# Where the group norm is scaled, and who ends the late rotary units, in an attention + RWKV + FFN kernel

## The reference, cut to what matters

```python
x = x + attn_a(layernorm(x))       # 16 heads of 16, rotary q and k, causal softmax
x = x + ffn(layernorm(x))          # int weights, 256 -> 768 -> 256, silu(gate) * up
x = x + attn_b(layernorm(x))       # RWKV-6, 4 heads of 64
x = x + ffn(layernorm(x))

def _apply_rope(t):                # q and k
    rot = concatenate([-t2, t1])   # the halves of each head, swapped
    return t * cos + rot * sin
# attn_b ends, per token and head, with a group norm, an affine map and a gate:
y = _wkv6(r, k, v, w, u)
y = (y - mean) / sqrt(var + eps)   # over the 64 channels of a head
y = y * ln_g + ln_b
out = (y * g) @ Wo
```

## Time and profile before

| | us |
|---|---|
| median of 3 runs | 3526.66 |
| lowest, highest | 3525.41, 3527.14 |
| the profiled execution's own time | 3525.63 |
| its span, first to last instruction | 3523.5 |

### The profile page before, as it was taken

One profiled execution on the slowest core, in us unless ns is written; L12 is line 12 of the kernel. 1 busy time (PEld: TensorE's weight loads), 2 busy tenths in 40 slices (PEclk: granted clock), 3 DMA queues, 4 the chain that ended last, 5 costly groups with the idle time before them and its releaser, 6 DMA issues.

```text
span 3523.5 us, 47199 instructions
## 1 busy us (share of the span) xinstructions
PE 2997.0 (85%) x17056; PEld 1840.7 (52%) x17056; DVE 2507.5 (71%) x5137; ACT 1309.5 (37%) x2721; POOL 1308.2 (37%) x1244
## 2 busy tenths in 40 slices
PE   2588889889888898888988888888888888898898
PEld 1236565365743567345763447535475364653667
DVE  5676687677775867857778577785687756876665
ACT  1263223722346232453225531265313642236322
POOL 0023551235512454124641346213462234522355
PEclk9699999999999999899998999899998999999999
DMA  4600033000410006000150002400023000330000
GB/s 133 105 2 13 19 61 56 1 13 19 79 39 10 14 10 97 20 14 10 25 101 2 14 9 46 80 2 13 18 46 71 2 13 19 49 68 2 1 1 13
DMA packets 68887, 115.04 MB, mean 33 GB/s; under 512 B 10795, under 2 KB 64075, under 8 KB 65531
## 3 DMA queue, kind: packets, MB, share of 16 engines
q1 hardware_dynamic: 68627, 111.51, 15.9%
HBM read 74.69 MB, written 33.65 MB: 31 GB/s over the span
## 4 chain that ended last, share of the span: by engine, by line
PE 49%; DVE 34%; POOL 5%; issue 4%; ACT 4%; DMA 2%; SPq 0%; DVEq 0%; POOLq 0%; ACTq 0%
DVE mxp L928 9%; PE PB L1266 7%; PE PB L1251 5%; PE PB L1326 5%; PE PB L1341 5%; PE PB L1237 4%; DVE arena L1111 4%; PE PB L1411 3%; PE PB L1380 3%; DVE attn L851 3%; PE PB L1299 3%; DVE arena L1120 2%; ACT arena L699 2%; DVE stats L840 2%; PE PB L1450 2%
## 5 line engine op out<-in xcount | busy, mean ns | idle before, releaser
L928 DVE TENSOR_REDUCE mxp<-PB 128x1 f32<-128x512 f32 (+3 forms) x1536 | 751.3, 547 | 155.4 <-PE PB L1237 85.2
L699 ACT ACTIVATE arena<-PB 128x512 f32<-128x512 f32 (+3 forms) x1536 | 649.3, 508 | 450.2 <-PE PB L1251 443.7
L1237 PE MATMUL PB<-arena 96*128 96x512 bf16 (+3 forms) x1536 | 508.4, 359 | 105.8 <-DVE mxp L928 64.8
L563 POOL TENSOR_SCALAR_AFFINE_SELECT arena<-arena 128x512 f32<-128x512 f32 x256 | 163.3, 638 | 996.8 <-ACT arena L699 996.5
L1251 PE MATMUL PB<-arena 99*128 99x512 bf16 (+3 forms) x1536 | 463.8, 342 | 26.8 <-DMA arena<-augT 19.5
L1237 PEld LDWEIGHTS PB<-arena 96*128 96x128 bf16 x1536 | 154.2, 101 | 424.8 <-DVE mxp L928 329.8
L1266 PE MATMUL PB<-arena 128*32 128x512 f32 (+3 forms) x3072 | 339.4, 514 | 15.5 <-ACT attn L688 13.7
L1326 PE MATMUL PB<-xh,wgu 128*128 128x512 f32 x768 | 314.1, 409 | 42.0 <-DVE xl L995 27.5
L573 POOL TENSOR_TENSOR hl<-arena,hh 128x512 fp32r<-128x512 f32 x192 | 248.3, 1295 | 240.5 <-ACT hh L724 236.4
L1326 PE MATMUL PB<-xl,wgu 128*128 128x512 f32 x768 | 310.2, 404 | 2.4 <-issue 2.4
L1486 PE MATMUL PB<-arena 128*128 128x128 f32 x1792 | 233.3, 281 | 59.4 <-DVE arena L1111 49.7
(11 more groups left out here) (139 smaller groups left out, 5367.4 us busy)
## 6 DMA issues: line engine op xcount, KB each, us to landing
arena<-parts SPq DMA_DIRECT2D x112, 256.0 KB, 9.7
parts<-arena SPq DMA_DIRECT2D x192, 128.0 KB
arena<-parts SPq DMA_DIRECT2D x16, 768.0 KB, 18.2
arena<-in_x SPq DMA_DIRECT2D x16, 512.0 KB, 4.0
arena<-parts SPq DMA_DIRECT2D x16, 512.0 KB, 20.4
xres<-in_x SPq DMA_DIRECT2D x16, 512.0 KB, 4.4
out<-xres SPq DMA_DIRECT2D x16, 512.0 KB, 4.1
wgu<-arena SPq DMA_DIRECT2D x2, 768.0 KB, 4.5
```

Of the source, the lines that this page charges most:

```text
L699: act.activation(pt[:, U % 3, h, 0:n], bank(b, "score", t)[:, 0:n], ACT.Exp, scale=DH ** -0.5).then_inc(act_emptied, 1)
L928: dve.reduce_max(mxp[:, g % 2, h, col:col + 1], bank(b, "max", g * NPC + k)[:, 0:n], axis=AX.X).then_inc(dve_emptied, 1)
L1237: last = mm(ps[:, 0:n], qst[0:AUG, h, 128 * i:128 * i + 128], kst[0:AUG, h, s0:s0 + n], start=True, stop=not diag)
```

## The change

1. Group norm: the multiplication with the reciprocal deviation goes from GpSimd (L634) to VectorE (`norm_scale`). VectorE's order becomes sums(0), then for each n: centre(n), sums(n+1), scale(n). GpSimd's order becomes: add and power of n, then plus ln_b and times the gate of n-1 (`norm_end`).
2. Units 4 to 7: VectorE does only the shuffle and the cosine product; the sine product and the sum go to GpSimd (`turn_in`), into four buffers of their own. At the start of the program GpSimd does them for sequence 0. Later, unit 4 stands before `ln_scale(3, b, 0)`, units 5 and 6 behind it, unit 7 behind `ln_scale(3, b, 1)`.
3. The split of units 4 to 7 moves out of the output projection into the last FFN: `high` before tiles 3, 5, 7 and 9, `mid` after the h part of tiles 4, 6, 8 and 11 on ScalarE; `remainder` after gates 4, 6, 8, 10, `low` after gates 7, 9, 11 and after the FFN on VectorE. SP's program is not changed.

```diff
+        turned_late = [halves(region(4096 + 512 * k, 512)) for k in range(4)]
...
@@ gpsimd
+                def turn_in(p, e):
+                    main, turned = ta[e % 4], turned_late[e - 4]
+                    sin = halves(rope[:, 1, HALF * (e // 2 % 2):HALF * (e // 2 % 2) + HALF])
+                    pool.wait_ge(rot_chain, 12 * p + e + 5)
+                    pool.tensor_tensor(turned, turned, sin, ALU.mult).then_inc(rot_sin, 1)
+                    pool.wait_ge(rot_sin, 4 * p + e - 3)
+                    wait_emptied(pool, p, "qk", e)
+                    pool.tensor_tensor(main, main, turned, ALU.add).then_inc(roped, 1)
+
                 ln_scale(0, 0, 0)
                 ln_scale(0, 0, 1)
+                for e in range(4, 8):
+                    turn_in(0, e)
...
+                    def norm_end(n):
+                        z = xn[:, 2 * n:2 * n + 2, :]
+                        pool.wait_ge(gn_scaled, 4 * b + n + 1)
+                        pool.tensor_tensor(z, z, lng[:, 1:2, :].broadcast_to([128, 2, D]), ALU.add).then_inc(gn_shifted, 1)
+                        pool.wait_ge(gn_shifted, 4 * b + n + 1)
+                        pool.tensor_tensor(z, z, gt[:, 2 * n:2 * n + 2, :], ALU.mult).then_inc(gn_gated, 1)
+
                     for n in range(4):
...
-                        pool.tensor_tensor(zh, zh, r, ALU.mult).then_inc(gn_chain, 1)
-                        pool.wait_ge(gn_chain, 12 * b + 3 * n + 1)
-                        pool.tensor_tensor(z, z, lng[:, 1:2, :].broadcast_to([128, 2, D]), ALU.add).then_inc(gn_chain, 1)
-                        pool.wait_ge(gn_chain, 12 * b + 3 * n + 2)
-                        pool.tensor_tensor(z, z, gt[:, 2 * n:2 * n + 2, :], ALU.mult).then_inc(gn_chain, 1)
+                        if n:
+                            norm_end(n - 1)
+                    norm_end(3)
+                    if ahead:
+                        turn_in(b + 1, 4)
                     ln_scale(3, b, 0)
+                    if ahead:
+                        turn_in(b + 1, 5)
+                        turn_in(b + 1, 6)
                     ln_scale(3, b, 1)
+                    if ahead:
+                        turn_in(b + 1, 7)
...
@@ scalar, in ffn
                             if e:
                                 h_part(e - 1)
+                            if k == 3 and ahead and e in (2, 4, 6, 8):
+                                high(b + 1, 3 + e // 2)
+                            if k == 3 and ahead and e in (5, 7, 9):
+                                mid(b + 1, (e + 3) // 2)
                         h_part(2 * NM - 1)
+                        if k == 3 and ahead:
+                            mid(b + 1, 7)
...
-                        if ahead and n % 2:
-                            high(b + 1, 4 + 2 * f)
-                            high(b + 1, 5 + 2 * f)
-                            mid(b + 1, 4 + 2 * f)
-                            mid(b + 1, 5 + 2 * f)
...
@@ vector, in rotary
+                    if e < 4:
+                        dve.wait_ge(rot_chain, 12 * p + 2 * e + 1)
+                        dve.tensor_tensor(turned, turned, sin, ALU.mult).then_inc(rot_chain, 1)
+                        wait_emptied(dve, p, "qk", e)
+                        dve.wait_ge(rot_chain, 12 * p + 2 * e + 2)
+                        dve.tensor_tensor(main, main, turned, ALU.add).then_inc(roped, 1)
...
@@ vector, in ffn
                             gate(k, s, e)
+                            if k == 3 and ahead and e in (4, 6, 8, 10):
+                                remainder(b + 1, 2 + e // 2)
+                            if k == 3 and ahead and e in (7, 9, 11):
+                                low(b + 1, (e + 1) // 2)
...
+                    def norm_scale(n):
+                        zh = xn[:, 2 * n:2 * n + 2, :].rearrange("p i (h j) -> p i h j", j=WH)
+                        r = grs[:, n % 2, :].rearrange("p (i h a) -> p i h a", i=2, a=1).broadcast_to([128, 2, 4, WH])
+                        dve.wait_ge(gn_rstd, 4 * b + n + 1)
+                        dve.wait_ge(gn_gained, 4 * b + n + 1)
+                        dve.tensor_tensor(zh, zh, r, ALU.mult).then_inc(gn_scaled, 1)
+
+                    norm_sums(0)
+                    for n in range(4):
+                        norm_centre(n)
+                        if n < 3:
+                            norm_sums(n + 1)
+                        norm_scale(n)
                     if ahead:
                         pair(rotary, b + 1, 4)
                     for n in range(4):
                         if n == 2 and ahead:
                             pair(rotary, b + 1, 6)
                         if n == 3:
-                            if ahead:
-                                pair(remainder, b + 1, 6)
                             x_low(3, 1, (0, 1))
                         residual("ob", n, 2)
-                        if n == 0 and ahead:
-                            pair(remainder, b + 1, 4)
-                        if n == 1 and ahead:
-                            pair(low, b + 1, 4)
                         if n % 2:
                             ln_half(3, n // 2)
+                    ffn(3, 1)
                     if ahead:
-                        pair(low, b + 1, 6)
-                    ffn(3, 1)
+                        low(b + 1, 7)
                     down(3, 2)
                     down(3, 3)
...
@@ tensor
-                        pe.wait_ge(gn_chain, 12 * b + 6 * f + 6)
+                        pe.wait_ge(gn_gated, 4 * b + 2 * f + 2)
```

More of the change, by code:

```diff
@@ L240, in ct, with halves @@
             return a.rearrange("p (c t) -> p c t", c=NC)
+        def halves(a):
+            return a.rearrange("p (a n) -> p a n", a=2)
         HIGH = 16384
@@ L307, in build @@
         rot_chain = sem("rot_chain")
+        rot_sin = sem("rot_sin")
         hi_done = sem("hi_done")
@@ L342, in build @@
         gn_rstd = sem("gn_rstd")
-        gn_lng = sem("gn_lng")
-        gn_chain = sem("gn_chain")
+        gn_gained = sem("gn_gained")
+        gn_scaled = sem("gn_scaled")
+        gn_shifted = sem("gn_shifted")
+        gn_gated = sem("gn_gated")
         stored = [sem(f"stored{f}") for f in (0, 1)]
@@ L874, in rotary @@
                     dve.tensor_tensor(main, ps, cos, ALU.mult).then_inc(dve_emptied, 1)
-                    dve.wait_ge(rot_chain, 16 * p + 2 * e + 1)
-                    dve.tensor_tensor(turned, turned, sin, ALU.mult).then_inc(rot_chain, 1)
-                    wait_emptied(dve, p, "qk", e)
-                    dve.wait_ge(rot_chain, 16 * p + 2 * e + 2)
-                    dve.tensor_tensor(main, main, turned, ALU.add).then_inc(roped, 1)
+                    if e < 4:
[4 more added lines that the diff above has]
+                        dve.tensor_tensor(main, main, turned, ALU.add).then_inc(roped, 1)
                 def remainder(p, e):
@@ L1135, in _, with norm_sums, norm_centre @@
                                 dve.engine_nop().then_inc(dve_emptied, 1)
-                    for n in range(4):
+                    def norm_sums(n):
                         wait_filled(dve, b, "y", n)
-                        if n >= 2:
-                            dve.wait_ge(gn_chain, 12 * b + 3 * (n - 2) + 1)
-                        ps = bank(b, "y", n)[:, :].rearrange("p (a j) -> p a j", j=WH)
-                        for a in range(8):
-                            dve.bn_stats(gst[:, a, :], ps[:, a, :]).then_inc(gn_stat, 1)
+                        for k in range(8):
+                            dve.bn_stats(gst[:, k, :], bank(b, "y", n)[:, WH * k:WH * k + WH]).then_inc(gn_stat, 1)
                         dve.wait_ge(gn_stat, 32 * b + 8 * n + 8)
-                        for a in range(8):
-                            dve.bn_aggr(gmv[:, n % 2, a, :], gst[:, a, :]).then_inc(gn_aggr, 1)
+                        for k in range(8):
+                            dve.bn_aggr(gmv[:, n % 2, k, :], gst[:, k, :]).then_inc(gn_aggr, 1)
+                    def norm_centre(n):
+                        z = xn[:, 2 * n:2 * n + 2, :]
                         dve.wait_ge(gn_aggr, 32 * b + 8 * n + 8)
-                        z = xn[:, 2 * n:2 * n + 2, :]
                         dve.tensor_tensor(z.rearrange("p i (h j) -> p i h j", j=WH),
```

13 lines of the change are left out of this document (3 added, 10 removed).

## The result

The changed kernel takes 3551.6 us (median of 7 runs, 3538.6 to 3557.6); beside it the kernel before took 3527.1 (7 runs, 3525.4 to 3530.8). The ratio is 1.0064, 95% interval 1.0048 to 1.0080: slower by 0.64%, some 23 us. The forecast was 3528, its own range 3520 to 3535, the wider one 3500 to 3550. The median lies 1.6 us above the wider one; taken by the ratio on the 3526.66 us of the table ahead, the changed kernel is at 3549.2, just inside it. The profiled execution took 3554.7 us, its span 3553.0; before it was 3523.5.

A forecast was written before the change was run, and what follows sets the result against it. No engine is full, so TensorE's waits for GpSimd, VectorE and augT's DMA count. Per sequence -3.7 + 0.5 + 3.45 = +0.25, seven give +1.8: profiled 3527.4, median 3528 us; own range 3520 to 3535, eight in ten 3500 to 3550.

The forecast's parts named there:

- gain and late DMA cancel: The forecast's own case: earlier FFN work and later augT offset each other, +0.25 us per sequence; chance 0.36.
- L1534's wait for GpSimd: Transposes of the normed rows wait for GpSimd's last multiply, 42.3 us in 9 waits; claimed to go.
- LN3's norm at the meeting: VectorE's LN3 norm coincides with GpSimd's unit end on shared ports: 3.2 us instead of 1.38 alone.
- x low done: VectorE delivers the low half of x for the last FFN's first matmuls at 936.7 instead of 941.5.
- work behind the second transposes earlier: Transposes of LN3's second half move from 946.95 to 943.2, 3.7 us earlier.
- last FFN longer from there: The split's added VectorE work in the last FFN costs 0.5 us in all, bounds 0 and 1.5.
- S earlier: S is the start of the next sequence's row maxima, 983.75 before; 3.7 us gained less 0.5 in the FFN.
- augT landed, first score starts: The row maxima's DMA, behind stack loads, output stores and x, lands at S + 32.9.
- the sum's last term: The augT DMA delays the next sequence's first score by 3.45 us, all paid; bounds 1 and 11.9.
- the second rival: Loads meet output stores and x, augT lands 7 us late, +3.8 a sequence: 3554; decides from 4.2; chance 0.22.
- Gain kept: Rival: VectorE wins the port or the queue clears early, 3.5 us a sequence: 3502, at bounds 3488; chance 0.33.
- The FFN rival: VectorE's 5.6 us backlog fills the bank ring in the last FFN, 2 us more a sequence: 3542; chance 0.09.

The follow-up runs named there:

- e1: The changed kernel with x's loads put behind the first augT DMA in SP's queue (sequences 1 to 7): 3514.1 us, ratio 0.9961.
- e3: The kernel before, with only SP's stack loads of heads 8 to 15 held back until late in the last FFN: 3580.8 us, ratio 1.0154.
- e7: The changed kernel with GpSimd's ends of units 5, 6 and 7 waiting until VectorE has done LN3's norms: 3516.9 us, ratio 0.9982.
- e8: The changed kernel with GpSimd kept off LN3's norms and x's loads behind the first augT in all eight sequences: 3483.1 us, ratio 0.9872.
- e4: The kernel before with only the split of units 4 to 7 moved into the last FFN: 3543.9 us, ratio 1.0049.
- e10: The kernel before with the split moved into the last FFN and x's loads behind the first augT: 3499.6 us, ratio 0.9918.
- e6: The kernel before with the group norm's edit and the rotation's ends on GpSimd, the split left in place: 3569.5 us, ratio 1.0121.
- e5: The kernel before with the group norm's edit alone: 3552.9 us, ratio 1.0072.
- e9: The kernel before with x's loads behind the first augT in all eight sequences: 3526.0 us, ratio 0.9993.

## Why the prediction was right or wrong

It forecast that gain and late DMA cancel. Its terms, and what they measured in sequence 1 (times of day have 2.11 us taken off, as above):

| step | forecast | measured |
|---|---|---|
| LN3's first reciprocal deviation on GpSimd | 928.2 | 927.1 |
| first transposes later | 2.1 us | 2.0 us |
| L1534's wait for GpSimd | gone | gone; 1.88 us at the first transposes instead |
| LN3's norm at the meeting | 3.2 us | 3.27 and 3.29 us |
| x low done | 936.7 | 935.5 |
| first gate, up matmuls earlier | some 5 us | 4.8 us |
| LN3's second norm done | 943.2 | 943.2 |
| work behind the second transposes earlier | 3.7 us | 3.8 us |
| last FFN longer from there | 0.5 us | 1.4 us |
| S earlier | 3.2 us | 2.4 us |
| stack loads issued | S - 2.1 | S - 2.3 |
| augT issued | S + 29.3 | S + 28.8 |
| augT landed, first score starts | S + 32.9 | S + 33.6 |
| later than before | 3.45 us | 4.05 us |
| TensorE at half speed behind that, to the output projection | no term | 2.3 us |
| the same, from there to the next group norm | no term | 2.1 us |
| sum per sequence (432.8 us against 426.6) | +0.25 us | +6.2 us |

The whole profiled execution (3553.0 against 3523.5 us of span), added up over the sequences from the start times of the same rows:

| stretch | before, us | after, us | difference | forecast |
|---|---|---|---|---|
| first y statistics to S, 7 times | 591.5 | 575.3 | -16.2 | -22.4 |
| S to the first score, 7 times | 206.7 | 234.0 | +27.3 | +24.2 |
| first score to output projection, 8 times | 967.2 | 977.3 | +10.1 | 0 |
| output projection to y statistics, 8 times | 1523.8 | 1535.2 | +11.4 | 0 |
| start to sequence 0's first score, and the last sequence from its y on | 234.4 | 231.2 | -3.2 | 0 |

**What held.** Each place named was the right one. The chain of waits moved as worked out: the group norm ends GpSimd's chain sooner, the meeting at LN3 eats most of what the rotation frees, the stack loads go out 28 us later, and augT stands behind them. The prediction left to the run which engine starts first and so, by the rule of the Trainium skill (SBUF — State Buffer, "Who interferes with whom"), keeps the ports: it is GpSimd, 929.22 against 929.35, and the trace agrees with the rule, with GpSimd at its usual 1.27 us and VectorE at 3.27. augT landed 3.5 us after its issue behind x, against 1.9 alone in the sequence's later loads.

**The step that failed is the sum's last term, augT "3.45 us late, all of it paid".** The lateness was read nearly right (3.9 us on average), but more than the lateness was paid. The sum stops at the first score and has no term for TensorE's clock. In the profiled execution the two stretches behind the first score, in which the change moves no work, are 21.5 us longer, with 37 us more of TensorE at half speed in them. The sum has this execution 1.8 us longer than before, and it is 29.5 us longer: of the 27.7 us between, these are 21.5, the smaller gain is 6.2, the longer wait 3.1, and the start and end take 3.2 off.

The price isn't the same each time. From group norm to group norm, two of the seven sequences are as the sum has it (-0.1 and +0.7 us against before; the forecast was +0.25), the other five are 3.5 to 7.0 us longer, with one or more drops to half speed that the kernel before doesn't have. In four pairs of kernels that differ only in the queue, the medians' ratios move by more than the waits do: 36 us for 29.5 us of waits (the kernel after and e1), 54 for 35.2 (before and e3), 39 for 24.7 (e7 and e8), 46 for 22.6 (e4 and e10). By their intervals these differences are uncertain by 7 to 9 us each, so the first pair alone wouldn't show it, the other three do: a later augT costs more than its wait. (The profiled executions of e7 and e8, one fast for its kernel and the other slow, differ by 26 us only.) Why a drop falls into one sequence and not into the next is not shown, and a late augT isn't its only cause: e1 has drops in four stretches where the kernel before has none, and e6 has them with augT on time.

**A smaller term was mis-sized: the FFN.** 0.5 us were forecast, 1.4 came, and so 3.2 us of gain became 2.4. It wasn't VectorE's backlog. TensorE waits 0.66 and 0.95 us for the pieces of the second norm, does seven transposes in 1.98 us and starts the second half's gates at half speed; the first six of these matmuls take 2.4 us (946.36 to 948.77) against 1.5 before (948.03 to 949.54):

```profile
948.03 0.50 PE L1326 MATMUL PB<-xh,wgu 128*128 128x512 f32 x1
```

The rest fits the waits for hl, which rose from 39.2 to 42.2 us over the span. That the second norm ended at 943.2 as forecast is in part luck: x low was done 1.2 us sooner than forecast, and VectorE's residual then waited 0.99 us for an output projection that TensorE did at half speed (3.48 us; 938.64 above), for which the prediction had no term.

**The rivals.** The late DMA turned it slower, as the second rival said, and its 3554 is nearly the time. That is luck: it reached it by 7 us of lateness and would have let 4.05 pass (its own point was 4.2). The clock made up the difference. "Gain kept" fell on both its conditions. e8, which keeps the two engines apart and puts augT ahead of x, shows what it is worth when the meeting and the lateness are gone: 0.9872, 3483 us, 5 us under its bound of 3488. The FFN rival's cause, VectorE, didn't show: TensorE's waits for VectorE's gates (L1361 for L1034) are 5.5 us, 6.3 before.

**What the parts are worth.** By ratios, on 3527 us: group norm alone +25, with the rotation +43, the split alone +17, all three +23; with x behind augT, the split alone -29 and all three -14; with the meeting gone too -45. The split alone brings S 3.3 us forward, all three 2.4: with the meeting in, the first two parts cost 0.9 us. The group norm's edit removed the longest visible wait and was priced at a small gain; alone it is a loss of 25 us, since VectorE carries the stage. The prediction didn't see this, because the third part's relief of VectorE (four remainders and lows out of the stage) was in the same sum.

**Open.** Why the sequences of the kernel after take 427 to 434 us from group norm to group norm and not one value was not settled. Its 7 runs spread over 19 us; those of before over 5 us beside it and up to 13 us beside the experiments. That the last sequence is 3.3 us shorter from its y on (the prediction had 0, at most 2) is explained by the group norm's edit for 1.4 us only (e5).

## What to carry to other kernels

A wait beside which TensorE runs at half speed can cost more than its length: read the granted clock on both sides, and far behind it, before you price a later arrival (in the four pairs here it cost 1.2 to 2.0 times the wait). When a producer's end moves later, follow every queue it issues into up to the next small transfer behind it; the mend was a few lines of order in SP's queue, worth some 36 us in the changed kernel and nothing in the kernel before. Before moving work onto the engine that a wait names as not late, ask who sets the stage's end without that wait; and keep the other of VectorE and GpSimd off a short chain that everyone waits for, by one semaphore, even if it makes that engine idle.

## What the runs showed of the hardware

- A chain of four VectorE instructions of 0.35 us each took 3.27 us beside two GpSimd operations of 1.27 us that read SBUF, of which the first had started 0.13 us ahead. Both chains together ran from 929.22 to 932.62, 3.4 us, where one wholly behind the other would be 1.38 + 2.53 = 3.9. Over the run this made line 874's 192 instructions 130.7 us instead of 104.2.
- 8 KB loads of augT landed in 1.9 us with nothing before them in the queue, 3.5 us behind 1 MB of x, 12.4 us behind the stacks and x at the start, 8.1 to 11.3 us behind the stacks alone (e9): its place in the queue is what such a transfer costs.
- What a wait costs beyond its length, where TensorE is at half speed on both sides of it, isn't fixed. With 1.1 us of idle the return to 2.4 GHz came 4.8 to 4.9 us behind the first score in all seven later sequences before; with 3.9 to 5.9 us of idle it came after 3.7 to 6.4 us, and in five of seven sequences further drops to half speed followed, some over 100 us later.
